# Gate products on four column groups, in pairs of batches, with selector zeros and weight pieces moved

## The reference

```python
q = layernorm(x); k = v = ctx_1024
ifg = concat([q, k, v])                      # 768 features
ig = (ifg @ igate_w.T + igate_b).T           # 8 heads x 512
fg = (ifg @ fgate_w.T + fgate_b).T
cs = cumsum(log_sigmoid(fg))
log_D = mask(cs[:, :, None] - cs[:, None, :]) + ig[:, None, :]
D_mat = exp(log_D - max(log_D))
C = (q_h @ k_h.T / sqrt(32)) * D_mat
h = C @ v_h / (max(abs(sum(C)), exp(-max(log_D))) + eps)
x = x + tanh(g_xattn) * layernorm(h) * ln_scale
x = x + tanh(g_ffn) * experts(layernorm(x))  # top 2 of 9, hidden 704
```

## Time and profile before

| | us |
|---|---|
| median of 3 runs (778.26 to 780.39) | 779.48 |
| the profiled execution, its time | 777.09 |
| its span, first to last instruction | 775.3 |
| TensorE busy | 663.8 (86%) |
| VectorE busy | 516.8 (67%) |
| GpSimd busy | 409.1 (53%) |
| ScalarE busy | 386.7 (50%) |

### The profile page before, as it was taken

The page is one execution under the profiler, slowest core; times in us unless marked ns, Lnnn a source line. Parts: engine busy times, 40 slices in busy tenths (PEclk is TensorE's granted clock), DMA queues, the critical chain, the costliest instruction groups (busy, mean ns, idle before and its releaser), DMA issues.

```text
span 775.3 us, 18373 instructions
## 1 busy us (share of the span) xinstructions
PE 663.8 (86%) x6306; PEld 532.0 (69%) x6306; DVE 516.8 (67%) x1371; ACT 386.7 (50%) x973; POOL 409.1 (53%) x401
## 2 busy tenths in 40 slices
PE   2982989998988953278999999999999999999993
PEld 1541546665665542157889989988989899899893
DVE  7715898999899968945565655565556555555561
ACT  4443677888787761444444433444434344444340
POOL 5025599999999970031454352444443625444423
PEclk9995555556557555579999999999999999999997
DMA  9814789997998851352887797988977968879752
GB/s 282 281 37 125 212 272 272 317 288 241 291 315 277 265 183 30 145 204 94 267 280 251 230 317 204 266 286 245 298 243 230 318 205 274 284 226 301 236 136 47
DMA packets 85820, 179.74 MB, mean 232 GB/s; under 512 B 14881, under 2 KB 48546, under 8 KB 85730
## 3 DMA queue, kind: packets, MB, share of 16 engines
q1 hardware_dynamic: 63202, 140.10, 56.7%
q0 software_dynamic: 13824, 18.43, 11.2%
q10 hardware_dynamic: 8704, 20.06, 6.6%
HBM read 140.93 MB, written 38.67 MB: 232 GB/s over the span
## 4 chain that ended last, share of the span: by engine, by line
PE 54%; POOL 19%; DVE 10%; issue 8%; DMA 4%; ACT 2%; SPq 1%; POOLq 0%; DVEq 0%; ACTq 0%
PE bank L1091 45%; POOL whl L479 8%; DMA out<-res,TS 3%; POOL x L712 3%; POOL vp L560 2%; POOL qE L576 2%; PE bank L298 2%; POOL x L715 2%; PE bank L301 2%; PE bank L1085 1%; POOL kw L568 1%; DVE R L986 1%; PE bank L311 1%; DVE xl L1147 1%; DMA EB<-e_d 1%
## 5 line engine op out<-in xcount | busy, mean ns | idle before, releaser
L1091 PE MATMUL bank<-xh,w 128*128 128x256 bf16 (+1 forms) x1760 | 266.5, 262 | 9.7 <-DVE xl L1147 9.7
L1073 POOL DMA_INDIRECT out<-res,TS x72 | 115.3, 1602 | 213.9 <-DVE res L1208 107.1
L1091 PE MATMUL bank<-xl,w 128*128 128x256 bf16 (+1 forms) x880 | 221.8, 262 | 0.0
L1164 ACT ACTIVATE sg<-bank 128x256 f32<-128x256 f32 (+1 forms) x240 | 86.8, 362 | 228.4 <-PE bank L1091 228.4
L1091 PEld LDWEIGHTS bank<-xh,w 128*128 128x128 bf16 x1760 | 165.0, 98 | 27.9 <-issue 11.9
L1194 DVE TENSOR_TENSOR hf<-sg,bank 128x256 f32<-128x256 f32 (+1 forms) x200 | 78.9, 395 | 115.7 <-ACT sg L1164 115.7
L1091 PE MATMUL bank<-w,hh 128*128 128x256 bf16 x864 | 140.0, 273 | 0.0
L479 POOL TENSOR_TENSOR whl<-wst,whl 128x408 bf16<-128x408 f32 x96 | 94.9, 1015 | 46.7 <-ACT whl L464 46.1
L1064 POOL DMA_INDIRECT xg<-y_d,TG x72 | 72.1, 1002 | 78.9 <-DVE TS L1021 48.4
L1091 PE MATMUL bank<-w,hlo 128*128 128x256 bf16 x360 | 98.1, 273 | 0.0
L1158 ACT CAST hh<-hf 128x256 bf16<-128x256 f32 (+1 forms) x240 | 90.3, 376 | 12.5 <-DVE hf L1196 12.5
(11 more groups left out here) (218 smaller groups left out, 1058.9 us busy)
## 6 DMA issues: line engine op xcount, KB each, us to landing
w<-w_d SPq DMA_DIRECT2D x40, 1408.0 KB, 9.1
w<-w_d SPq DMA_DIRECT2D x40, 768.0 KB, 4.6
wst<-in_wts SPq DMA_DIRECT2D x32, 612.0 KB, 5.8
w_d<-whl ACTq DMA_DIRECT2D x32, 612.0 KB, 7.2
vb<-in_kv SPq DMA_DIRECT2D x8, 528.0 KB, 5.0
xa<-in_x SPq DMA_DIRECT2D x8, 512.0 KB, 8.3
kT<-in_kv SPq DMA_DIRECT2D x8, 512.0 KB, 8.9
xc<-in_x SPq DMA_DIRECT2D x8, 512.0 KB, 8.1
```

The source lines that it names most:

```text
L1073: nc.gpsimd.indirect_dma_start(out, bass.IndirectOffsetOnAxis(ap=TS[:, c0:c0 + 1], axis=0), res[w][:, j, :], None, bounds_check=TOK - 1, o ...
L1091: mm = nc.tensor.matmul(dst, l, r, start=(n == 0), stop=(n == len(pairs) - 1))
L1164: nc.scalar.activation(sg[m % 2][0:K, 0:N], bank[0:K, 2 + (NM * w + m) % 4, 0:N], ACT.Silu).then_inc(f_sg, 1)
```

## The change

- `a_pe_gates` takes a pair of batches, n and n + 4, which stand next to each other in the new order `ORDER`. Each product of 128 output rows is replaced by two of 32 rows, one for the forget and one for the input gate. Four of them, two batches by two gates, write rows 0, 32, 64 and 96 of `GATES`, each on its own group of 32 columns of the array, and are issued one behind the other. Products over `kT` stand ahead of the wait for `qT`, as before.
- TensorE does two turns, then the gates of the pair. SyncE loads two `xa` first, then the small tables, then two `kT` and two `xa` in turn.
- The zeros of `mx` are written in 16 pieces and the ones of `asb` in four; the selector is copied in 16 pieces, two behind each batch's `qT` copies.
- On GpSimd `w_pool(1)` moves behind `g_pool`; on ScalarE `w_hi_act(1)` moves behind the first store, `w_hi_act(2)` and the second store behind `b_vh_act(0)`. SyncE's `w_sync(2)` and `w_sync(3)` stay ahead of `g_sync`.

```diff
             for w in range(2):
-                nc.gpsimd.memset(mx[w][:, :, :, :], 0.0).then_inc(s_mz, 1)
-                nc.gpsimd.memset(asb[w][:, :, :], 1.0).then_inc(s_mz, 1)
+                for q in range(2 * HG):
+                    nc.gpsimd.memset(mx[w][:, q // HG, q % HG, :], 0.0).then_inc(s_mz, 1)
+            for w in range(2):
+                for g in range(2):
+                    nc.gpsimd.memset(asb[w][:, g, :], 1.0).then_inc(s_mz, 1)
...
-        def mx_act(act, w):
-            act.wait_ge(s_mz, 2 * w + 1)
-            nc.scalar.copy(mx[w][0:12, :, :, :], sel12[:, :].unsqueeze(1).unsqueeze(3).to_broadcast([12, 2, HG, S])).then_inc(s_sel, 1)
+        def mx_act(act, i):
+            w = i // HG
+            for q in (i % HG * 2, i % HG * 2 + 1):
+                act.wait_ge(s_mz, w * 2 * HG + q + 1)
+                nc.scalar.copy(mx[w][0:12, q // HG, q % HG, :], sel12[:, q % HG:q % HG + 1].to_broadcast([12, S])).then_inc(s_sel, 1)
...
+        ORDER = (0, 4, 1, 5, 2, 6, 3, 7)
+
+        def a_stats_dve(dve, i):
+            n = ORDER[i]
             ge(dve, a_x[n], 16)
             for c in range(NC):
                 nc.vector.bn_stats(stA[:, n * NC + c, :], xa[n][:, c, :]).then_inc(a_st, 1)
-            ge(dve, a_st, n * NC + NC)
+            ge(dve, a_st, i * NC + NC)
...
+        def a_qn_dve(dve, i):
+            n = ORDER[i]
+            ge(dve, a_rs, i + 1)
+            ge(dve, a_tr, i * 2 - 2)
...
-        def a_pe_gates(pe, n):
-
-            o = BH - n * NH
-            ge(pe, a_k[n], 16)
+        def a_pe_gates(pe, p):
+            pair = (ORDER[2 * p], ORDER[2 * p + 1])
+
+            def tiles4(row, src, k, stop):
+                for first, col0 in ((0, BH), (BH, 2 * BH)):
+                    for n in pair:
+                        o = col0 - n % 4 * NH
+                        q = first + n // 4 * 32
+                        mm = nc.tensor.matmul(GATES[q:q + 32, :], wwin[:, row, o:o + 32], src[:, n, :, k * P:(k + 1) * P],
+                                              start=False, stop=stop)
+                return mm
+
+            for n in pair:
+                ge(pe, a_k[n], 16)
             for k in range(KD):
-                nc.tensor.matmul(GATES, wwin[:, KD + k, o:o + P], kT[:, n, :, k * P:(k + 1) * P], start=False, stop=False)
-            ge(pe, a_qt, n * 2 + 2)
+                tiles4(KD + k, kT, k, False)
+            ge(pe, a_qt, p * 4 + 4)
             for k in range(KD):
-                mm = nc.tensor.matmul(GATES, wwin[:, k, o:o + P], qT[:, n, :, k * P:(k + 1) * P], start=False,
-                                      stop=(n == NB - 1 and k == KD - 1))
+                mm = tiles4(k, qT, k, p == NB // 2 - 1 and k == KD - 1)
             mm.then_inc(a_gp, 1)
...
-            act.wait_ge(a_gp, NB)
+            act.wait_ge(a_gp, NB // 2)
             nc.scalar.activation(g1[:, :], GATES[0:BH, :], ACT.Abs).then_inc(g_act, 1)
             act.wait_ge(g_act, 1)
             nc.scalar.activation(g2[:, :], g1[:, :], ACT.Exp, scale=-1.0).then_inc(g_act, 1)
             act.wait_ge(g_act, 2)
             nc.scalar.activation(g3[:, :], g2[:, :], ACT.Ln, bias=one_c[0:BH, 0:1]).then_inc(g_act, 1)
             w_store(act, 0)
-            w_store(act, 1)
-            w_hi_act(act, 2)
+            w_hi_act(act, 1)
...
-            a_x_sync(sp, 0)
+            a_x_sync(sp, ORDER[0])
+            a_x_sync(sp, ORDER[1])
             sp.dma_start(wg[:, :, :], wgate).then_inc(s_small, 16)
             sp.dma_start(fib_s[:, :], fib).then_inc(s_small, 16)
             sp.dma_start(lnr[:, :], lnrow).then_inc(s_small, 16)
             sp.dma_start(gs[:, :], gsc).then_inc(s_small, 16)
             sp.dma_start(wr[:, :, :], wroute).then_inc(s_small, 16)
             sp.dma_start(rb[:, :], rbias).then_inc(s_small, 16)
-            for n in range(1, NB):
-                a_x_sync(sp, n)
-                a_k_sync(sp, n - 1)
-            a_k_sync(sp, NB - 1)
+            for p in range(NB // 2):
+                for n in ORDER[2 * p:2 * p + 2]:
+                    a_k_sync(sp, n)
+                for n in ORDER[2 * p + 2:2 * p + 4]:
+                    a_x_sync(sp, n)
...
-            mx_act(act, 0)
             a_norm_act(act, 0)
             for n in range(NB):
                 if n < NB - 1:
                     a_norm_act(act, n + 1)
                 a_qt_act(act, n)
-                if n == 2:
-                    mx_act(act, 1)
+                mx_act(act, n)
             w_hi_act(act, 0)
-            w_hi_act(act, 1)
             g_actf_all(act)
             b_vh_act(act, 0)
+            w_hi_act(act, 2)
+            w_store(act, 1)
             b_exp_act(act, 0)
             b_ch_act(act, 0)
...
             pool.wait_ge(s_lsg, 1)
-            for n in range(2):
-                w_pool(pool, n)
+            w_pool(pool, 0)
             g_pool(pool)
+            w_pool(pool, 1)
             b_v_pool(pool, 0)
             pool.wait_ge(g_cols, 2)
...
-            a_pe_turn(pe, 0)
-            pe.wait_ge(s_wwin, 4)
-            for n in range(NB):
-                if n < NB - 1:
-                    a_pe_turn(pe, n + 1)
-                a_pe_gates(pe, n)
+            for p in range(NB // 2):
+                a_pe_turn(pe, 2 * p)
+                a_pe_turn(pe, 2 * p + 1)
+                if p == 0:
+                    pe.wait_ge(s_wwin, 4)
+                a_pe_gates(pe, p)
```

More of the change, by code:

```diff
@@ L261, in a_stats_dve, with a_norm_act, a_qt_act @@
                 nc.vector.bn_stats(stA[:, n * NC + c, :], xa[n][:, c, :]).then_inc(a_st, 1)
-            ge(dve, a_st, n * NC + NC)
+            ge(dve, a_st, i * NC + NC)
             for c in range(NC):
                 nc.vector.bn_aggr(mvA[:, n * NC + c, :], stA[:, n * NC + c, :]).then_inc(a_mv, 1)
-        def a_qn_dve(dve, n):
-            ge(dve, a_rs, n + 1)
-            ge(dve, a_tr, n * 2 - 2)
+        def a_qn_dve(dve, i):
+            n = ORDER[i]
+            ge(dve, a_rs, i + 1)
+            ge(dve, a_tr, i * 2 - 2)
             for c in range(NC):
                 t = n * NC + c
-                nc.vector.tensor_scalar(qn[(n % 2) * NC + c][:, :], xa[n][:, c, :], mvA[:, t, 0:1], rsA[:, t:t + 1],
+                nc.vector.tensor_scalar(qn[(i % 2) * NC + c][:, :], xa[n][:, c, :], mvA[:, t, 0:1], rsA[:, t:t + 1],
                                         ALU.subtract, ALU.mult).then_inc(a_q, 1)
-        def a_norm_act(act, n):
+        def a_norm_act(act, i):
+            n = ORDER[i]
             ts = slice(n * NC, (n + 1) * NC)
-            ge(act, a_mv, n * NC + NC)
+            ge(act, a_mv, i * NC + NC)
             nc.scalar.activation(lvA[:, ts], mvA[:, ts, 1], ACT.Ln, bias=eps_c[:, 0:1]).then_inc(a_lv, 1)
-            ge(act, a_lv, n + 1)
+            ge(act, a_lv, i + 1)
             nc.scalar.activation(rsA[:, ts], lvA[:, ts], ACT.Exp, scale=-0.5).then_inc(a_rs, 1)
-        def a_qt_act(act, n):
+        def a_qt_act(act, i):
+            n = ORDER[i]
             for v in range(2):
-                ge(act, a_tr, n * 2 + (v + 1))
+                ge(act, a_tr, i * 2 + (v + 1))
                 nc.scalar.copy(qT[:, n, 2 * v:2 * v + 2, :].rearrange("p c d -> p (c d)"),
-                               bank[:, 2 * (n % 2) + v, :]).then_inc(a_qt, 1)
+                               bank[:, 2 * (i % 2) + v, :]).then_inc(a_qt, 1)
         GATES = bank[:, 4, :]
@@ L291, in a_pe_bias, with a_pe_turn @@
             nc.tensor.matmul(GATES, fib_s[0:1, :], ones_row[0:1, :], start=True, stop=False)
-        def a_pe_gates(pe, n):
-            o = BH - n * NH
-            ge(pe, a_k[n], 16)
+        def a_pe_gates(pe, p):
[10 more added lines that the diff above has]
+                ge(pe, a_k[n], 16)
             for k in range(KD):
-                nc.tensor.matmul(GATES, wwin[:, KD + k, o:o + P], kT[:, n, :, k * P:(k + 1) * P], start=False, stop=False)
-            ge(pe, a_qt, n * 2 + 2)
+                tiles4(KD + k, kT, k, False)
+            ge(pe, a_qt, p * 4 + 4)
             for k in range(KD):
-                mm = nc.tensor.matmul(GATES, wwin[:, k, o:o + P], qT[:, n, :, k * P:(k + 1) * P], start=False,
-                                      stop=(n == NB - 1 and k == KD - 1))
+                mm = tiles4(k, qT, k, p == NB // 2 - 1 and k == KD - 1)
             mm.then_inc(a_gp, 1)
-        def a_pe_turn(pe, n):
+        def a_pe_turn(pe, i):
             for v in range(2):
-                ge(pe, a_q, n * NC + (2 * v + 2))
-                ge(pe, a_qt, n * 2 + (v - 3))
+                ge(pe, a_q, i * NC + (2 * v + 2))
+                ge(pe, a_qt, i * 2 + (v - 3))
                 for j in range(2):
                     for k in range(KD):
-                        mm = nc.tensor.transpose(bank[:, 2 * (n % 2) + v, (2 * j + k) * P:(2 * j + k + 1) * P],
-                                                 qn[(n % 2) * NC + 2 * v + j][:, k * P:(k + 1) * P], identf[:, :])
```

(6 more changed lines are left out.)

1 line of the change is left out of this document (removed).

## The result

The changed kernel takes 769.37 us (median of 4 runs, 768.45 to 770.07) against 779.50 in the same comparison: ratio 0.9858, 95% interval 0.9832 to 0.9883, so 1.4% faster. Run again later, against 778.74, it took 770.47, ratio 0.9883 (0.9854 to 0.9911). The profiled execution took 770.07 us, span 768.2, against 777.09 and 775.3. The prediction was 768.9 in a range of 763 to 776.

The account below looks back on a forecast made before the run. Ahead of the first decay product at 74.1 us, TensorE bounds the gates, then a dependent chain follows. Gates 16.0 us earlier less 5.4 us store delay gives 10.6, so 779.5 becomes 768.9 us, range 763 to 776.

Parts of the forecast that it names:

- The gates: Front stage up to the first gate activation, called G: start moves from 56.1 to 40.1 us, range 38 to 43.
- The second turn: TensorE's second batch of transposes in the front stage, bound by data and VectorE: ends at 17.0 us.
- The half-clock loss: First pair's gate products on TensorE, until the clock rises: 0.2 to 1.9 us lost, 1.3 taken.
- the waits for ScalarE: TensorE idle before the second half of a pair's gates: 0.73 us in two pairs, 0.35 in the last, 1.8 taken.
- The start: Front stage up to the first `qn`: starts near 11.5 us instead of 15.9; fills may cost up to 1 us.
- the delay of the stores: Gate-stage stores queued on SyncE behind the load waiting for GpSimd's second piece: 5.4 us late, range 4.9 to 6.7.
- Hidden work: Weight pieces moved on ScalarE cost nothing, 1.2 us if their cover were gone; the GpSimd piece costs GpSimd nothing.
- The later stages: Stretch from the first decay product (`dl`) to the end: stays as long as before, 701.2 us.
- No SyncE cost: Rival on the gate-stage stores: SyncE's wait costs nothing, time 763.5 us; chance 0.10.
- Two at once: Rival on the gate products: two run together, not four, gates stay 27.5 us, time 780, no change; chance 0.07.
- none at once: Rival on the gate products: none run together, gates take 55 us, time 806, slower; chance 0.03.
- Clock falls: Rival on the front stage: TensorE's clock drops, partly giving 776 us (chance 0.09) or wholly giving 784 (0.05).

Follow-up runs that it names:

- zeros later: Changed kernel with GpSimd's zeros of the second `mx` tile and the ones of `asb` held back until later `qn` work; 767.1 us.
- load 3 behind: Changed kernel with SyncE's load of weight piece 3 moved from ahead of the gate-stage stores to behind the EB loads; 766.7 us, ratio 0.981 to the kernel before.
- wide products: Changed kernel with the 128-row gate products put back, pairs and all else kept; 783.6 us, ratio 1.004 to the kernel before.
- same group first: Changed kernel with both k products of one column group issued next to each other, then those of the next group; 771.1 us.
- pieces back: Changed kernel with the weight pieces on GpSimd and ScalarE in the order of the kernel before; 765.6 us, ratio 0.979 to the kernel before.
- groups without pairs: Kernel before with each 128-row gate product split into two of 32 rows, batch by batch, no pairs, nothing else moved; 783.0 us.
- all mended: Changed kernel with late zeros, selector pieces in ScalarE's idle times, piece 0 converted before the last turn, old piece order; 762.8 us, ratio 0.979 to the kernel before.

## Why the prediction was right

**The gates, 56.1 to 40.1: measured 40.03.** The column groups ran four at once, at 0.43 us a pass of 512 columns, so 16 x 0.86 us stood as predicted. The Trainium skill ("TensorE: Matmul & The Clock Gate", "Measured speedup vs the span model") gives 3.07 times for four packed row tiles; by it a group would have taken 1.12 us, an estimate. Here sixteen passes, two groups, took 1.82 us, 0.91 a group with a mode change in it, so for column tiles in a stream the measurement decides. The exact hit of the sum is partly luck, since its errors cancel. The second turn ended at 18.0, not 17.0. The half-clock loss was 0.5, not 1.3, because the clock rose soon after the second four; the waits for ScalarE were 0.6, 0.3 and 0.15, 1.0 in all against 1.8; turns and mode changes took 6.3 against 6.0, with a wait of 0.3 for `qn` in them. When the clock rises differs from run to run: the first sixteen passes took 2.26 us in this profile and 3.42 in the changed kernel's second one, and G lay at 40.0 and 41.3. And G was not TensorE's alone: ScalarE came free at the same moment.

**The start.** I had written that the fills might cost the first `qn` up to 1 us. They cost 1.3 (12.33 against 11.02 in zeros later), and by a way that I had not seen: fills of 0.51 us stood end to end, and the copy at 7.53 got no turn between them but waited for the last. Zeros later shows this cause, by taking the fills away.

**The step that was too small: the delay of the stores, 5.4 for 6.7 us**, just at the end of its range. The mechanism was right: SyncE's in-order queue held eight stores behind the load that waits for piece 1. Two terms were short and one was not needed. The piece took 3.22 us instead of 2.78, which released SyncE at G + 13.5 instead of 12.9. From there to the start of the last store it took 6.2 us instead of 4.9, with stores of 1.08 and 1.32 us where I had 0.59 and 0.45, beside the transfers of two weight pieces. The 0.5 us for a slower landing did not come: from the last store to dl it was 5.0 us, as before. And one sentence was wrong though it cost nothing here: "the scans' own pace is unchanged". VectorE's part got 2.7 us longer (`mp` complete at G + 15.2 instead of G + 12.5), nearly all of it in the two instructions that ran beside GpSimd's piece. It lay hidden behind the SyncE wait, and load 3 behind uncovered it. So the forecast's one cause was real, but taking it away alone gives back 3.2 of the 6.7 us.

**Hidden work.** ScalarE's moved conversions and stores show no cost in these rows, as said. The GpSimd piece itself "cost it nothing" on GpSimd, but it did cost on VectorE.

**The later stages.** dl moved by 9.3 us, the span by 7.1. A later stage that changes its length was one of the prediction's signs of being wrong, and here it is 2.2 us longer. Most of that fits one row of the windows above: from 345 to 352 us the granted clock was 0.76, in the first expert steps, where before it held at 1.00; that is 1.7 us of work at full clock. Profiles with such a dip (changed, wide, same group, pieces back, groups without pairs, all mended) have 702.8 to 704.7 us from dl to the end, those without 700.6 to 701.7. It isn't of the change: the changed kernel's second profile has 701.7. That the time was met within 0.5 us is luck in part: the profiled execution came at 770.1 where the prediction had 766.5, 1.3 us of it by a later dl and 2.2 by the later stages. The prediction carried over from before that the profiled execution lies 2.4 us below the median; here it lay 0.7 above, and that took back the 3.1 us. So the medians show 10 us and the two profiles 7, with 9.3 at dl between them.

**A reading.** The prediction names GpSimd as the fullest engine from 74 to 300 us. Its have VectorE at 197.6, GpSimd at 196.1 and TensorE at 196.0 us, so three engines share that place. Nothing in the sum hangs on it.

**The rivals.** No SyncE cost: refuted by load 3 behind. Two at once and none at once: refuted by the timeline, and wide products gives the size, 11.8 us of G. Clock falls: once it had risen, the passes kept 0.43 us until G in both profiles of the changed kernel. The Trainium skill ("TensorE: Matmul & The Clock Gate", "Part 4: PE-mode transpose") says that a transpose doesn't count as activity for the clock in the same way. Here the clock did not fall over 1.9 us of transposes in a row and 0.6 us of wait. In all mended even two turns with the wait of 1.69 us between them, from 26.60 to 30.82, left it up: the next sixteen passes took 1.75 us. So stretches as short as these gave no reason to fear for it.

## What to carry to other kernels

Four products of 32 output rows on four column groups cost nearly what one of 128 rows costs (0.91 us against 0.86), so zero-padded windows that add into one bank are worth taking apart, once four independent products stand in the list together; two give nothing. When a step is moved on one engine, look for who waits for its semaphore in every in-order queue: here a load nobody needed yet held eight stores that everybody needed. Moving the load behind them gave 2.7 us (766.7 against 769.4), and moving GpSimd's piece as well 7 in all (762.2). And after taking a wait away, ask what was late behind it; here that was the second half.

## What the runs showed of the hardware

- Products on free column groups started past a product that waited for its own group: sixteen passes of four groups took 1.9 us with both products of a group next to each other (same group first), and 1.82 in the changed kernel's order. Whether TensorE or an earlier step put them in that order, the traces don't show.
- A change between full-width and column-group work costs 0.1 to 0.15 us: in groups without pairs, with two changes a batch, a batch takes 4.58 us instead of 4.31.
- GpSimd fills held some of VectorE's instructions and not others. A copy of 128x16 took 4.30 us behind nine fills that stood end to end, and 0.17 without them. The statistics of the first `xa` ran from 4.76 among fills at their usual 1.4 us, and `revj` took 0.18 us at 4.16. The runs don't show what decides it.
- Beside a GpSimd `tensor_tensor` a VectorE `tensor_tensor` of 64x512 took 3.46 us instead of 1.63, and a scan of 64x512 1.98 instead of 1.22 (pieces back).
- In six of the eleven profiles of these kernels at the usual clock the granted clock falls in the first expert steps (0.76 on average from 345 to 352 us in the changed kernel's), and their time from dl to the end is about 2 us longer. What share this has in the differences between runs of one kernel is not shown; the kernel before alone ran from 776.96 to 785.60 us in one comparison.
